# mLSTM gates worked out pair by pair, the value product moved to VectorE, and GpSimd's first products of the second pair released earlier

## What is computed

```python
q = x @ Wq + bq;  k = (x @ Wk + bk) * inv_sqrt_d;  v = x @ Wv + bv
i_pre, f_pre, o_pre = jnp.split(x @ Wg + bg, 3, axis=-1)
log_i = softcap(i_pre + input_bias)          # 10 * tanh(. / 10)
log_f = -jax.nn.softplus(f_pre)
def step(carry, inp):
    m_next = jnp.maximum(lf + m, li)
    i_s = jnp.exp(li - m_next);  f_s = jnp.exp(lf + m - m_next)
    M = f_s[:, :, None] * M + i_s[:, :, None] * (vt[:, :, None] * kt[:, None, :])
    n = f_s * n + i_s * kt
    h_raw = jnp.einsum('bij,bj->bi', M, qt)
    denom = jnp.maximum(jnp.abs(jnp.einsum('bi,bi->b', n, qt))[:, None], 1e-06)
    h = jax.nn.sigmoid(op) * (h_raw / denom)
```

## Time and profile before

| | before |
|---|---|
| median of 3 runs | 1097.47 us (1096.16 to 1099.6) |
| the profiled execution's own time | 1096.09 us |
| its span, first to last instruction | 1094.1 us |
| mean granted TensorE clock | 0.729 of full speed |
| busy: PE, DVE, ACT, POOL | 837.4, 802.2, 516.2, 548.8 us |

### The profile page before, as it was taken

One profiled execution on the slowest core, in us unless ns is written; L12 is line 12 of the kernel. 1 busy time (PEld: TensorE's weight loads), 2 busy tenths in 40 slices (PEclk: granted clock), 3 DMA queues, 4 the chain that ended last, 5 costly groups with the idle time before them and its releaser, 6 DMA issues.

```text
span 1094.1 us, 11522 instructions
## 1 busy us (share of the span) xinstructions
PE 837.4 (77%) x3813; PEld 357.3 (33%) x3813; DVE 802.2 (73%) x1046; ACT 516.2 (47%) x1014; POOL 548.8 (50%) x357
## 2 busy tenths in 40 slices
PE   7782366586956898894888887788888887878887
PEld 4441134464924232441212111111111111114566
DVE  1246799866543234368999999999999999994366
ACT  1364330166344564575555555555555444445621
POOL 0010567730010000001999999999999999980100
PEclk9986576668656899897566677766667567569876
DMA  9000000610100000001100110110011011000001
GB/s 389 31 1 0 1 0 0 133 37 0 59 0 1 1 1 1 1 1 42 42 25 18 43 36 16 33 42 18 25 42 27 15 43 37 6 0 1 1 15 27
DMA packets 20504, 33.08 MB, mean 30 GB/s; under 512 B 10078, under 2 KB 19294, under 8 KB 19422
## 3 DMA queue, kind: packets, MB, share of 16 engines
q1 hardware_dynamic: 20446, 32.36, 10.5%
HBM read 17.57 MB, written 1.20 MB: 17 GB/s over the span
## 4 chain that ended last, share of the span: by engine, by line
PE 39%; DVE 31%; issue 12%; ACT 11%; POOL 4%; SPq 1%; DMA 1%; DVEq 0%; ACTq 0%; POOLq 0%
DVE pair_arrays L1586 14%; DVE pair_arrays L1570 5%; PE PS L748 4%; ACT pair_arrays L895 4%; PE PS L720 3%; PE PS L730 3%; PE PS L420 3%; ACT PS L895 3%; PE PS L574 3%; PE PS L840 2%; PE PS L510 2%; DVE pair_arrays L1392 2%; PE PS L481 2%; PE PS L866 2%; ACT token_weights L895 2%
## 5 line engine op out<-in xcount | busy, mean ns | idle before, releaser
L1250 POOL TENSOR_TENSOR pair_arrays<-pair_arrays 128x736 f32<-128x736 f32 x192 | 332.1, 1743 | 24.8 <-DVE pair_arrays L1586 24.5
L895 ACT ACTIVATE PS<-PS,A_negative 128x368 f32<-128x368 f32 x384 | 191.3, 538 | 130.0 <-PE PS L730 129.5
L1586 DVE TENSOR_TENSOR_SCAN pair_arrays<-PS,scan_carry,pair_arrays 128x368 f32<-128x368 f32 x256 | 235.8, 964 | 0.6 <-ACT PS L895 0.4
L1570 DVE TENSOR_TENSOR pair_arrays<-pair_arrays,PS 128x736 f32<-128x736 f32 x144 | 129.0, 895 | 8.6 <-PE PS L720 8.4
L748 PE MATMUL PS<-pair_arrays,weights 128*32 128x368 f32 x768 | 130.7, 704 | 1.5 <-POOL pair_arrays L1250 1.4
L1202 POOL TENSOR_TENSOR big<-pair_arrays 128x1104 f32<-128x1104 f32 (+15 forms) x32 | 55.9, 1768 | 141.5 <-DVE pair_arrays L1346 68.6
L1586 DVE TENSOR_TENSOR_SCAN pair_arrays<-PS,pair_arrays 128x368 f32<-128x368 f32 x128 | 110.3, 904 | 2.1 <-ACT PS L895 2.1
L720 PE MATMUL PS<-spread_rows,token_weights 96*128 96x368 bf16 x192 | 64.3, 428 | 37.9 <-DVE pair_arrays L1570 23.5
L1258 POOL TENSOR_TENSOR pair_arrays<-pair_arrays,token_weights 128x736 f32<-128x736 f32 x48 | 83.9, 1748 | 18.5 <-ACT token_weights L895 18.5
L720 PE MATMUL PS<-pair_arrays,token_weights 96*128 96x368 bf16 x192 | 69.9, 461 | 27.0 <-DVE pair_arrays L1570 21.2
L481 PE MATMUL PS<-big,weights 128*128 128x368 f32 (+15 forms) x192 | 61.8, 489 | 31.1 <-DVE big L1403 20.7
(11 more groups left out here) (190 smaller groups left out, 1260.3 us busy)
## 6 DMA issues: line engine op xcount, KB each, us to landing
big<-in_x SPq DMA_DIRECT2D x4, 2048.0 KB, 17.5
big<-decay_rows SPq DMA_DIRECT2D x4, 1104.0 KB, 15.7
spread_rows<-pair_arrays SPq DMA_DIRECT2D x96, 46.0 KB, 2.0
pair_arrays<-pair_arrays SPq DMA_DIRECT2D x96, 46.0 KB, 1.9
spread_rows<-big SPq DMA_DIRECT2D x48, 46.0 KB, 1.9
pair_arrays<-big SPq DMA_DIRECT2D x48, 46.0 KB, 1.9
weights<-in_wts SPq DMA_DIRECT2D x1, 2204.0 KB, 18.1
big<-in_wexp SPq DMA_DIRECT2D x1, 1536.0 KB, 7.9
```

The lines of the kernel that those rows point to most:

```text
L895: return nc.scalar.activation(o, i, fn, **kw)
L1250: nc.gpsimd.tensor_tensor(hcbuf[t % NRING], hbuf[t % NRING], c4(seg).unsqueeze(1).to_broadcast([128, 2, G]), ALU.mult).then_inc(s("hc_read ...
L1570: tt(bx[t % NRING], b4(seg).unsqueeze(1).to_broadcast([128, 2, G]), PS[:, 2:4, 0:G], ALU.mult).then_inc(s("b_used"), 1)
L1586: nc.vector.tensor_tensor_scan(hbuf[t % NRING][:, h, :], PS[:, 4 + 2 * (t % 2) + h, 0:G], bx[t % NRING][:, h, :], carry[:, a:a + 1] if k e ...
```

## The change

What is done to the gates of both pairs at once is cut into functions of a pair. On ScalarE the softplus of the first pair goes ahead of `gates(1)`, that of the second pair behind it, with the tables for exp and ln loaded by name in between, and the four exps of `factors` follow pair by pair. On VectorE the gate arithmetic of the first pair is put between the evacuations of the second pair; that of the second pair follows them, and then come i times k, the scan for n and n times q for one pair after the other. The product of v and i goes from GpSimd to the end of that on VectorE. GpSimd's lag products 1 and 3 wait for the evacuations alone.

```diff
@@ ScalarE, gates(p)
-                if p == NPAIR - 1:
-                    act.wait_ge(s("gates_ev"), (p * 3 + 2) * NG)
-                    step(f(fs, fs, ACT.Exp, scale=-1.0))
-                    f(lf, fs, ACT.Ln, bias=ONE).then_inc(s("softplus"), 1)
...
+            def softplus(p):
+                act.wait_ge(s("gates_ev"), (p * 3 + 2) * NG)
+                step(f(fs[:, p, :], fs[:, p, :], ACT.Exp, scale=-1.0))
+                f(lf[:, p, :], fs[:, p, :], ACT.Ln, bias=ONE).then_inc(s("softplus"), 1)
+            def factors(p):
+                act.wait_ge(s("exponents"), 2 * p + 1)
+                f(fs[:, p, :], fs[:, p, :], ACT.Exp).then_inc(s("factors"), 1)
+                act.wait_ge(s("exponents"), 2 * p + 2)
+                f(li[:, p, :], li[:, p, :], ACT.Exp).then_inc(s("factors"), 1)
...
+            softplus(0)
             gates(1)
-            act.wait_ge(s("exponents"), 1)
-            f(fs, fs, ACT.Exp).then_inc(s("factors"), 1)
-            act.wait_ge(s("exponents"), 2)
-            f(li, li, ACT.Exp).then_inc(s("factors"), 1)
+            exp_ln_tables()
+            softplus(1)
+            for p in range(NPAIR):
+                factors(p)
@@ GpSimd
             pool.wait_ge(s("qkv_ev"), 3 * NGR)
-            pool.wait_ge(s("exponents"), 2)
             lag_product(1)
             lag_product(3)
-            pool.wait_ge(s("factors"), 2)
-            nc.gpsimd.tensor_tensor(v_, v_, li, ALU.mult).then_inc(s("iv_ready"), 1)
@@ VectorE
+            def gate_sums(p):
+                dve.wait_ge(s("gates_ev"), (p * 3 + 2) * NG)
+                step(ts(li[:, p, :], li[:, p, :], 10.0, None, ALU.mult))
+                dve.wait_ge(s("softplus"), p + 1)
+                step(stt(lf[:, p, :], lf[:, p, :], -1.0, r_[:, p, :], ALU.mult, ALU.subtract))
+            def gate_max(p):
+                step(nc.vector.tensor_tensor_scan(m_[:, p, :], lf[:, p, :], li[:, p, :], 0.0, ALU.add, ALU.max))
+            def gate_forget(p):
+                nc.vector.tensor_copy(fs[:, p, 0:1], lf[:, p, 0:1])
+                step(tt(fs[:, p, 1:], lf[:, p, 1:], m_[:, p, 0:SP - 1], ALU.add))
+                tt(fs[:, p, :], fs[:, p, :], m_[:, p, :], ALU.subtract).then_inc(s("exponents"), 1)
+            def gate_input(p):
+                tt(li[:, p, :], li[:, p, :], m_[:, p, :], ALU.subtract).then_inc(s("exponents"), 1)
@@ VectorE, qkv(p), behind the evacuation of kind r, column group k
+                        if p and (r, k) == (0, 2):
+                            gate_sums(0)
+                        if p and (r, k) == (1, 1):
+                            gate_max(0)
+                        if p and (r, k) == (2, 0):
+                            gate_forget(0)
+                        if p and (r, k) == (2, 2):
+                            gate_input(0)
@@ VectorE, behind qkv(1)
+            gate_sums(1)
+            gate_max(1)
+            gate_forget(1)
+            gate_input(1)
             for p in range(NPAIR):
+                dve.wait_ge(s("factors"), 2 * p + 2)
+                tt(ik[:, p, :], li[:, p, :], k_[:, p, :], ALU.mult).then_inc(s("ik_ready"), 1)
+                dve.wait_ge(s("ik_ready"), p + 1)
                 step(nc.vector.tensor_tensor_scan(n_[:, p, :], fs[:, p, :], ik[:, p, :], 0.0, ALU.mult, ALU.add))
                 tt(ik[:, p, :], n_[:, p, :], q_[:, p, :], ALU.mult).then_inc(s("nq_ready"), 1)
+            tt(v_, v_, li, ALU.mult).then_inc(s("iv_ready"), 1)
```

More of the change, by code:

```diff
@@ L1184, in forward_decays @@
             def forward_decays():
-                pool.wait_ge(s("ik_ready"), 1)
+                pool.wait_ge(s("ik_ready"), NPAIR)
                 pool.wait_ge(s("iv_ready"), 1)
@@ L1363, in _ @@
             qkv(1)
-            dve.wait_ge(s("gates_ev"), 3 * NGR - NG)
-            step(ts(li, li, 10.0, None, ALU.mult))
-            dve.wait_ge(s("softplus"), 1)
-            step(stt(lf, lf, -1.0, r_, ALU.mult, ALU.subtract))
+            gate_sums(1)
+            gate_max(1)
+            gate_forget(1)
+            gate_input(1)
             for p in range(NPAIR):
-                step(nc.vector.tensor_tensor_scan(m_[:, p, :], lf[:, p, :], li[:, p, :], 0.0, ALU.add, ALU.max))
-            nc.vector.tensor_copy(fs[:, :, 0:1], lf[:, :, 0:1])
-            step(tt(fs[:, :, 1:], lf[:, :, 1:], m_[:, :, 0:SP - 1], ALU.add))
-            tt(fs, fs, m_, ALU.subtract).then_inc(s("exponents"), 1)
-            tt(li, li, m_, ALU.subtract).then_inc(s("exponents"), 1)
-            dve.wait_ge(s("factors"), 2)
-            tt(ik, li, k_, ALU.mult).then_inc(s("ik_ready"), 1)
-            dve.wait_ge(s("ik_ready"), 1)
-            for p in range(NPAIR):
+                dve.wait_ge(s("factors"), 2 * p + 2)
+                tt(ik[:, p, :], li[:, p, :], k_[:, p, :], ALU.mult).then_inc(s("ik_ready"), 1)
+                dve.wait_ge(s("ik_ready"), p + 1)
                 step(nc.vector.tensor_tensor_scan(n_[:, p, :], fs[:, p, :], ik[:, p, :], 0.0, ALU.mult, ALU.add))
                 tt(ik[:, p, :], n_[:, p, :], q_[:, p, :], ALU.mult).then_inc(s("nq_ready"), 1)
+            tt(v_, v_, li, ALU.mult).then_inc(s("iv_ready"), 1)
             dve.wait_ge(s("den_ev"), NGR)
```

## The result

The median goes from 1098.53 us (1096.16 to 1100.02, four runs) to **1084.22 us** (1081.68 to 1086.71, four runs): a ratio of 0.987, with an interval of 0.9846 to 0.9894. The profiled execution of the changed kernel happens to be the longest of its four, at 1086.71 us, with a span of 1084.5.

The account below looks back on a forecast made before the run. VectorE's gate arithmetic, behind a stretch where it mostly idles, bounds the stage. 94.2 + 20.07 + 4.88 = 119.15 us for the second n times q, against 131.10, gives 11.95 us less: median 1085.5 us, range 1080 to 1091.5.

Parts of the forecast that it names:

- The third evacuation: VectorE's third evacuation of the second pair: forecast at 82.7 us instead of 80.86, behind the first pair's softplus on ScalarE.
- The inserts don't stop the rounds: First pair's gates, 7.31 us, between VectorE's evacuations: banks refill meanwhile, VectorE doesn't wait, evacuations end at 94.2 us.
- The rival at 99.3: Inserts on VectorE delay TensorE and ScalarE too: evacuations end at 99.3, not 94.2; total 1090.6 us; chance 0.14.
- The second softplus: Second pair's softplus on ScalarE behind the sigmoids: over at 95.4 us, hidden from VectorE by 0.8 us.
- Behind the evacuations: VectorE's work from last evacuation to second n times q: 20.07 us, plus 4.88 for GpSimd.
- GpSimd's term: GpSimd's lag products 1 and 3 take turns with VectorE behind the evacuations: all 4.88 us added.
- The rival by which GpSimd costs nothing: GpSimd's two lag products find gaps beside VectorE: 4.88 us less, total 1080.6 us; chance 0.10.
- The value product: On GpSimd it cost 4.88 us; on VectorE, 2.46 us behind the last n times q, it costs nothing.
- the two cases that were given for the room around it: Spare time around the value product in VectorE's wait: 1.2 us, or about 0.6 if TensorE's sums took half the time.
- Behind the lag loop's start: Later stages are released by TensorE's sums, so the gain, 11.95 us at second n times q, carries through unchanged.
- the forecast's sign of being wrong: The forecast is wrong if, among other signs, the lag loop takes longer than before.
- the fourth rival: Expert stage: TensorE's clock rises later and the kernel gets slower; 17.8 us more, 1103.3 us; chance 0.03.

Follow-up runs that it names:

- gates_after: The changed kernel with the first pair's gates on VectorE all behind the evacuations, ahead of the second pair's; 1086.82 us, ratio 0.9885.
- no_reads: The changed kernel with GpSimd's lag products 1 and 3 replaced by memsets that write constants into the same columns; 1080.76 us, ratio 0.9838.
- no_value: The changed kernel with the value product cut to 8 of each pair's 1104 columns; 1083.12 us, ratio 0.9867.
- products_late: The changed kernel with GpSimd's lag products 1 and 3 held back until the second pair's exponents; 1084.72 us, ratio 0.987.
- changed_again: The changed kernel measured once more without any edit, as yardstick for the other runs; 1083.81 us, ratio 0.9865.
- sums_earlier: The changed kernel with the pieces of the first pair's gates one or two evacuations earlier on VectorE; 1084.1 us, ratio 0.9866.
- before_value: The kernel before the change with only the value product moved from GpSimd to VectorE, behind the last n times q; 1092.4 us, ratio 0.9951.
- sums_earlier_again: The changed kernel with the first pair's gates one or two evacuations earlier, the same edit measured a second time; 1083.64 us, ratio 0.9876.

## Why the prediction was right

*The third evacuation* was put at 82.7 and came at 82.80. The cost of the softplus at the front was sized rightly, 2.32 us against 1.11 + 1.22. The ends of the two tanh were misread on the way (79 and 81.3; the rows say 78.33 + 1.24 = 79.57 before and 80.58 + 1.02 = 81.60 after), which left the shift nearly the same.

*The inserts don't stop the rounds.* Forecast end of the evacuations 94.2, measured 93.68. The six behind the inserts come in twos of 1.10 to 1.11 us, not 1.20, which is 0.3 of the 0.5 us. The rival at 99.3 is out, and gates_after shows what the inserts are worth, 4.47 us.

*The second softplus* ends at 94.16 + 1.22 = 95.38, forecast 95.4, and nobody waits for it: log f starts at 97.90. But 2.34 of these 2.52 us are GpSimd's stretch of the times-10, so without GpSimd the cover would be 0.2 us, thinner than the 0.8 that was said, because VectorE arrived earlier. The two runs with earlier gates met it as a wait of 0.84 us. The two exps end at 97.40 and are asked for at 107.65.

*Behind the evacuations* 20.07 + 4.88 = 24.95 us were forecast and 24.16 measured. GpSimd's term was 0.48 too large; which of its gaps took that was not tried. The other 0.31 is VectorE's own instructions. That VectorE pays for nearly the whole of GpSimd's time, 4.88 us, was the less obvious step, and three runs hold it: it pays 4.40, 4.18 and 4.25 us (3.51 + 4.51 less 1.31 + 2.46 in gates_after) on three different pairs of instructions, and in no_reads 0.71. The rival by which GpSimd costs nothing, 1080.6, is near what no_reads made by force, 1080.76.

*The value product* costs nothing, as forecast: no_value shows it. Of the two cases that were given for the room around it, the thinner one came, 0.63 us, since the sums ran faster. That the figure fits is luck: it was given for sums done in half the time, and they took 2.40 us in place of some 3.2. In products_late, where they took 3.71, the room was 1.95. Its old place was sized at 4.88 us; measured from the two sides it is 4.67 and 4.45.

*Behind the lag loop's start* the forecast carried the gain through unchanged. This step was only nearly right, since the stages behind differ from execution to execution. In the profiled one the lag loop gave back 0.9 us, by the meeting of GpSimd and VectorE shown under changed_again, where the loop is 0.3 shorter than before; so the forecast's sign of being wrong, a longer lag loop, is not a loss of the change. In the same execution TensorE's clock gave back 1.7 us between the state scans and 1.9 in the expert stage; the latter is the mechanism of the fourth rival at about a tenth of its 17.8. The profiled execution, forecast at 1084.1 us, took 1086.71, though the second n times q was 1.3 us earlier than forecast.

*The median* is 14.3 us lower. The stage around the change makes 14.0 of it, at the lag loop's start. Of this 0.7 is the faster sums ahead of the loop, which the forecast didn't have and products_late didn't get. The lag loop takes back 0.9 in the first profile and nothing in changed_again. Added to the gain are the 1.5 us of those executions in which the rounds begin late, which only the kernel before pays; how many of the runs those are is not known. Why the median shows no loss to the clock has its answer in the profiles of all runs: the stretch from the first bf16 product of the expert stage to the layer norm behind it took 76.54 to 76.56 us in ten of twelve, and 78.4 in two, the first profile of the changed kernel and sums_earlier. Between the two state scans the loss is steadier: 26.33 to 26.39 us in the three profiles of the kernel before and before_value, 26.57 to 29.18 in the nine of the others. The mean granted clock there is 0.81 to 0.87 in the nine profiles up to 26.95 and 0.65 to 0.76 in the three of 28 and more. Whether the shorter gates themselves make the clock rise later there, or nine chances find more than three, stays open; nothing was run that sets the clock alone.

So the 13.25 us up to the second n times q are made of 2.26 from evacuations that end sooner though they carry 7.2 us of gates, and 10.99 behind them: those gates, 7.23, the exp wait of 2.11, and GpSimd's turns (6.95 before, 4.40 now, so 2.55), less 0.9 that the smaller pieces cost.

## What to carry to other kernels

Where an engine that sets the end waits in small pieces for a round of others, put later arithmetic of its own into the round in pieces as long as a few rounds; here 7.2 us of it cost 2.6. The products that GpSimd made beside VectorE's arithmetic were paid by VectorE nearly in full (4.2 to 4.7 us of 4.8 to 4.9), wherever they were released, unless VectorE was waiting anyway; so the thing to ask is which engine has a wait of that length, not when the product can start. And look at the thinnest cover (here 0.2 us of softplus, if GpSimd is left out) before moving a step further the same way.

## What the chip showed that was not expected

GpSimd's writes alone can hold VectorE: in no_reads the times-10, an operation with one input, took 1.43 us in place of 0.72 beside the second memset. The two-input subtraction ahead of it (95.31) took its quiet 1.30 beside the first, and neither memset was stretched (1.02 us for 1104 columns, 0.96 for 1035). In the changed kernel, where GpSimd's products read, the first product, which meets that subtraction and the times-10, took 3.52 us in place of 2.44, and the times-10 and log f took 3.06 and 3.37. The Trainium skill (SBUF — State Buffer, "Who interferes with whom") says that a VectorE instruction with two SBUF inputs contends with a GpSimd instruction that reads SBUF, not with one that only writes it, and that tensor_scalar can enter a mode in which it contends with GpSimd for the shared ports. These rows agree with both halves.

The same six sums took 2.40 us in one execution and 3.71 in another, the granted clock being 1.00, or 0.50 for the first 2 us, in kernels whose second n times q ends within 0.2 us of one another. A step of 1.6 us, as in sums_earlier_again, can thus be taken back ahead of the lag loop, and the loop itself varied by more than that over the changed kernel and its variants: its wait of the earlier trace rows came 64.2 to 68.3 us after its start.
